# Two-layer language-model tower: when the latent loop sums and centres its query weights, and in which order MHA turns the halves of its probabilities

## The reference

```python
# MHA: 8 heads of width 128
q, k, v = x @ Wq + bq, x @ Wk + bk, x @ Wv + bv
attn = softmax(q @ k.T / sqrt(128));  out = concat(attn @ v) @ Wo
# latent: 8 groups x 16 heads, 100 latent positions in each
xn = l2norm(x) * gamma
q = xn @ Wq_w + Wq_b                       # 128 heads of width 128
qk = q @ kc.T / sqrt(128);  att = softmax(qk)   # over the 100 positions of kc
z = att @ vc;  zn = l2norm(z) * wz_g1
h1 = silu(zn @ wz_w1 + wz_b1);  out = silu(l2norm(h1) * wz_g2 @ wz_w2 + wz_b2)
```

## Time and profile before

| | us |
|---|---|
| median of 3 runs | 3082.61 (lowest 3079.25, highest 5605.95) |
| the profiled execution, its own time | 3107.84 |
| its span | 3106.0 |
| mean granted PE clock in it | 0.948 of full speed |
| MHA's steps in it | about 756 to 1290 us |
| the latent loop in it | about 1361 to 3106 us |

### The profile page before, as it was taken

The page is one execution under the profiler, slowest core; times in us unless marked ns, Lnnn a source line. Parts: engine busy times, 40 slices in busy tenths (PEclk is TensorE's granted clock), DMA queues, the critical chain, the costliest instruction groups (busy, mean ns, idle before and its releaser), DMA issues.

```text
span 3106.0 us, 44621 instructions
## 1 busy us (share of the span) xinstructions
PE 2780.7 (90%) x14652; PEld 2264.8 (73%) x14652; DVE 2293.7 (74%) x4039; ACT 1750.1 (56%) x3398; POOL 2094.3 (67%) x1520
## 2 busy tenths in 40 slices
PE   0569989696999999779999999999999999999996
PEld 0437666595888888568888888888777787788875
DVE  1459989535666666568888888888888888888875
ACT  0269978334656656435555655555555555555553
POOL 5369978103777777527777777777777776777763
PEclk7589999798999999879999999999999999999997
DMA  1011100000000000100111111011010100111100
GB/s 46 22 35 27 27 21 16 28 1 28 1 1 1 1 1 1 63 17 33 44 34 44 34 37 39 34 44 45 32 34 32 44 32 33 46 37 34 45 19 7
DMA packets 44693, 87.01 MB, mean 28 GB/s; under 512 B 10677, under 2 KB 24781, under 8 KB 43825
## 3 DMA queue, kind: packets, MB, share of 16 engines
q1 hardware_dynamic: 42928, 81.00, 8.0%
q0 software_dynamic: 1536, 3.15, 0.4%
HBM read 64.44 MB, written 1.05 MB: 21 GB/s over the span
## 4 chain that ended last, share of the span: by engine, by line
PE 39%; DVE 6%; POOL 6%; issue 4%; ACT 0%; POOLq 0%; ACTq 0%; DVEq 0%
PE lat_ps_h L2173 15%; PE lat_ps_z L2184 8%; PE lat_ps_s L2123 7%; PE lat_ps_t L2152 6%; POOL lat_zz L1800 3%; POOL lat_wq L1763 2%; PE lat_ps_s L2139 2%; PE lat_ps_s L2130 2%; DVE lat_wq_sum L1857 1%; DVE latm_sc L1837 1%; DVE latm_top L1832 1%; DVE latm_attT L1852 1%; DVE latm_tot L1844 1%; POOL latm_att L1787 0%; PE lat_ps_s L2206 0%
## 5 line engine op out<-in xcount | busy, mean ns | idle before, releaser
L1787 POOL TENSOR_TENSOR latm_att<-latm_sc,latm_tot 128x500 f32<-128x500 f32 (+1 forms) x416 | 421.4, 1013 | 460.6 <-DVE latm_tot L1846 450.1
L2173 PE MATMUL lat_ps_h<-latm_attT,lat_share 125*128 125x512 f32 (+1 forms) x2472 | 681.1, 407 | 34.8 <-DVE latm_attT L1852 31.7
L1800 POOL TENSOR_TENSOR lat_zz<-lat_zz,lat_zsq 128x512 f32<-128x512 f32 x508 | 655.3, 1290 | 20.0 <-ACT lat_zsq L2030 12.7
L2023 ACT CAST latm_attT<-lat_ps_t 125x512 fp32r<-125x512 f32 (+1 forms) x512 | 301.8, 589 | 620.8 <-PE lat_ps_t L2152 620.8
L2173 PEld LDWEIGHTS lat_ps_h<-latm_attT,lat_share 125*128 125x128 f32 (+1 forms) x2472 | 461.7, 189 | 160.5 <-DVE latm_attT L1852 54.8
L2184 PE MATMUL lat_ps_z<-latm_attT,lat_vc 100*128 100x512 f32 x1536 | 485.5, 424 | 0.2 <-ACT lat_zsq L2030 0.2
L995 POOL TENSOR_SCALAR mha_probs<-mha_probs,mha_inv 128x1024 f32<-128x1024 f32 x128 | 364.6, 2849 | 121.7 <-DVE mha_inv L1216 121.5
L1852 DVE TENSOR_TENSOR latm_attT<-lat_ps_t,latm_attT 125x512 fp32r<-125x512 f32 (+1 forms) x512 | 348.5, 681 | 107.3 <-ACT latm_attT L2023 107.0
L2123 PE MATMUL lat_ps_s<-lat_wk,lat_xr 128*128 128x500 f32 (+1 forms) x1248 | 353.0, 392 | 12.3 <-DVE latm_sc L1837 5.5
L457 POOL TENSOR_TENSOR ret_probs<-ret_probs,ret_shared 128x1024 f32<-128x1024 f32 x128 | 306.1, 2425 | 49.3 <-ACT ret_probs L590 49.3
L2152 PEld LDWEIGHTS lat_ps_t<-ident,latm_att 128*125 128x125 f32 (+1 forms) x2048 | 284.2, 175 | 63.7 <-POOL latm_att L1787 16.6
(11 more groups left out here) (366 smaller groups left out, 4812.3 us busy)
## 6 DMA issues: line engine op xcount, KB each, us to landing
lat_w_in<-in_w_fives SPq DMA_DIRECT2D x52, 640.0 KB, 4.2
lat_wq_in<-in_wq_fives SPq DMA_DIRECT2D x52, 320.0 KB, 2.9
lat_share<-lat_share SPq DMA_DIRECT2D x200, 50.0 KB
ret_qk_head<-ret_qk_parts SPq DMA_DIRECT2D x256, 32.0 KB, 2.0
moe_w<-in_W SPq DMA_DIRECT2D x2, 1024.0 KB, 4.8
ret_shared<-in_xpos_q SPq DMA_DIRECT2D x1, 1024.0 KB, 5.6
ret_shared<-in_xpos_k SPq DMA_DIRECT2D x1, 1024.0 KB, 4.8
latw_wkv<-in_Wkv SPq DMA_DIRECT2D x1, 1024.0 KB
```

What stands on the lines that cost most here:

```text
L1787: nc.gpsimd.tensor_tensor(att[:, k % SLOTS].rearrange("p (j l) -> p j l", j=QH)[:, 0:n, 0:L], sc[:, u, 0:n * L].rearrange("p (j l) -> p j ...
L1800: nc.gpsimd.tensor_tensor(dst, dst, zsq[:, n % 2], ALU.add).then_inc(s["zz_added"], 1)
L2173: mm = e.matmul(ps_h[:, f, c, :], share[0:w, q % 2, w_part, cols], attT[0:w, n % 2, a_part], start=(n % NS in (0, QH) and (a_part, w_part) ...
```

## The change

Nothing is added or left out of the computation; instructions and waits move. In MHA, `turn`, `high` and `low` go through the two halves in the order 1, 0 in every step that follows a piece of keys or values (all odd steps), and PE's wait for that piece stands ahead of half 0 alone. In the latent loop the sum is two steps after the scaling (step 5, where it was 4) and the centring three (step 6, where it was 5). For the last five the scaling is two steps earlier, so that its sum is one step earlier and its centring too.

```diff
--- before.py
+++ after.py
@@ -960,6 +960,7 @@
         chunk = lambda c: slice(c * BANK, (c + 1) * BANK)
         makes_keys = lambda step: (step // TB + 1, step % TB // 2 - 1) if step < K - TB and step % TB in (2, 4) else None
         makes_values = lambda step: ((step + 2) // TB, (step + 2) % TB // 2) if TB <= step + 2 < K and (step + 2) % TB in (0, 2) else None
+        halves_of = lambda k: (1, 0) if makes_keys(k + 1) or makes_values(k + 1) else (0, 1)
 
         def closes(step):
 
@@ -1051,8 +1052,14 @@
             def turn(k):
 
                 e.wait_ge(s["normed"], START + k + 1)
-                for half in range(2):
+                for half in halves_of(k):
                     e.wait_ge(s[f"low_ready{half}"], START + k)
+                    if half == 0 and makes_keys(k + 1):
+                        n, c = makes_keys(k + 1)
+                        e.wait_ge(s["keys_ready"], START + 2 * n + c + 1)
+                    if half == 0 and makes_values(k + 1):
+                        n, i = makes_values(k + 1)
+                        e.wait_ge(s["v_full_ready"], START + 2 * n + i + 1)
                     for j in range(4):
                         mm = e.transpose(psT[:, half, j * P:(j + 1) * P], probs[:, k % 4, (4 * half + j) * P:(4 * half + j + 1) * P], ident[:])
                     mm.then_inc(s["turned"], 1)
@@ -1100,12 +1107,6 @@
             for step in range(K + 14):
                 if LAG <= step < K + LAG:
                     gather(step)
-                if step >= 1 and makes_keys(step - 1):
-                    n, c = makes_keys(step - 1)
-                    e.wait_ge(s["keys_ready"], START + 2 * n + c + 1)
-                if step >= 1 and makes_values(step - 1):
-                    n, half = makes_values(step - 1)
-                    e.wait_ge(s["v_full_ready"], START + 2 * n + half + 1)
                 for b, c in adds_out(step - 1):
                     e.wait_ge(s["out_added"], START + 2 * b + c + 1)
                 if 2 <= step <= K + 1:
@@ -1145,8 +1146,8 @@
                 n, i = k // TB, k % TB
                 if i % 4 == 0 and n > 0:
                     e.wait_ge(s[f"spent{i // 4}"], START + n)
-                for half in range(2):
-                    e.wait_ge(s["turned"], START + 2 * k + half + 1)
+                for nth, half in enumerate(halves_of(k)):
+                    e.wait_ge(s["turned"], START + 2 * k + nth + 1)
                     e.copy(probsT[:, 0, 4 * half:4 * half + 4, i * P:(i + 1) * P], psT[:, half, :].rearrange("p (j s) -> p j s", j=4)
                            ).then_inc(s[f"high_ready{half}"], 1)
 
@@ -1659,7 +1660,7 @@
             for q in range(1, FIVES):
                 for i in range(len(pieces(q))):
                     share_at[begins[q - 1] + ((1, 3) if q == FIVES - 1 else (3, 4, 8) if full(q - 1) else (1, 2, 4))[i]] = (q, i)
-            wq_at = {(begins[q - 1] - 7 if q > 1 else 1 - LEAD): q for q in range(1, FIVES)}
+            wq_at = {(begins[q - 1] - (9 if q == FIVES - 1 else 7) if q > 1 else 1 - LEAD): q for q in range(1, FIVES)}
             vc_at = {begins[q - 1] + (1 if full(q - 1) and q < FIVES - 1 else -1): q for q in range(1, FIVES)}
             width = lambda n: ROWS if full(steps[n][0]) and steps[n][2] < QH - 1 else L
             pieces_before = lambda q: sum(len(pieces(i)) for i in range(q))
@@ -1815,8 +1816,8 @@
                         scale_vc(vc_at[n])
                     if n in wq_at:
                         scale_wq(wq_at[n])
-                    if n - 2 in wq_at:
-                        centre_wq(wq_at[n - 2])
+                    if n - 3 in wq_at:
+                        centre_wq(wq_at[n - 3])
                     for i, b, c in due(n, "spread"):
                         spread_norm(i, c)
 
@@ -1973,8 +1974,8 @@
                         total(k)
                     if 0 <= n + 1 < K:
                         low(n + 1)
-                    if n - 1 in wq_at:
-                        mean_wq(wq_at[n - 1])
+                    if n - 2 in wq_at:
+                        mean_wq(wq_at[n - 2])
                     if n == -LEAD:
                         e.tensor_tensor(w2[:], w2[:], g2[:].unsqueeze(2).to_broadcast([P, 2, D]), ALU.mult).then_inc(s["g2_scaled"], 1)
                     for i, b, half in due(n, "norm"):
```

## The result

The changed kernel takes **3051.85 us** (median of 4 runs, 3051.02 to 3054.51) where the kernel before took 3082.11: a ratio of 0.9908, 95% interval 0.9894 to 0.9922, so about 28 us less (24 to 33). Forecast were 42.5 us less. The direction holds, a third of the gain is missing. The profiled execution took 3051.48 us; its span is 3049.7.

A forecast was written before the change was run, and what follows sets the result against it. PE, busy for 90% of the span, was taken as the bound. Latent loop 23.0, clock 3.4, last five 6.4, first sum 2.1 and MHA 7.6 sum to 42.5 us off 3082.61: 3040 us, range 3022 to 3052.

The forecast's parts named there:

- the regular fives: Latent loop, 38 of 48 fives: step 6 loses its 0.76 us wait, step 7 loses 0.28, so 0.48 us saved each.
- The ten fives: Latent loop, fives with further DVE work in step 4: that work delays as before, so the same 0.48 us saved each.
- The clock: Latent loop: PE's clock no longer falls after the two waits of 1.82 us, saving 3.4 us.
- The last five: End of latent loop: PE's 4.5 us wait for query weights and 1.9 us of lower clock go, saving 6.4 us.
- The first sum: First sum of query weights: DVE's idle time ahead of it gets filled with 2.10 us of work, saving 2.1 us.
- MHA: Attention: transposes of half 1 go ahead of PE's wait for a piece, hiding 28 short waits and part of two: 7.6 us.
- Centring a step later: Latent loop, POOL: costs nothing, as centring ends before make_wk needs it, with 2.3 us left as cover.
- the wait moves whole: Rival, latent loop: step 6's wait moves whole to step 7, DVE being the bound; 3066 us, chance 0.10.
- L1859 isn't held up: Rival, latent loop: L1859 takes 0.17 us, not held by POOL; 15.8 us more saved, 3024 us, chance 0.13.
- the swap that gains nothing: Rival, MHA: swapping halves gains nothing because the score behind then waits for the exponential; 3048 us, chance 0.09.
- MHA's rival: Rival, MHA: the swapped halves gain nothing, the score behind waiting for the exponential; 3048 us, chance 0.09.

The follow-up runs named there:

- one_input: The changed kernel without the division by the width and the query bias in the sum, so that L1860 reads one input: 3033.62 us, ratio 0.9838.
- between: The changed kernel with DVE's sum of query weights moved, within step 5, from behind low(6) to between shift and total: 3043.39 us, ratio 0.9887.
- mha_only: The kernel before with only the change's MHA part, the swapped halves: 3072.12 us, ratio 0.9965.
- early_sum: The changed kernel with scaling, sum and centring of all but one five two steps earlier (steps 1, 3 and 4): 3029.58 us, ratio 0.9834.

## Why the prediction was wrong

**What bounds the kernel, and the regular fives: right.** The wait in step 6 went, the new loss is in step 7 (3.47 us for 3.49 forecast), and a five gained 0.51 us for 0.48. The 0.68 us of L1860 and its end with L1801 came as worked out, and `one_input` and `between` show by two ways what being held costs: without it a five lasts 31.50.

**The step that failed:** "That work, 0.6 to 1.3 us, delays step 5 as before, and step 7 then by as much, where before it delayed step 6. So the same difference of 0.48 us is left." The work's duration was taken over from a place where the sum stood ahead of it and POOL was through. Without the sum it starts about 1.8 us sooner (measured from `low(5)`), inside POOL's instructions, and is itself held: the root 15.9 us for 7.0, and in the four other fives L1932 1.65 us for 1.21, L1948 1.14 and 1.11 for 0.68, L1949 1.67 and 1.65 for 0.69. I had the measure of this in hand for L1859, and applied it to the one instruction that the diff moves, not to those that it exposes. L1883, L1884, L1932, L1948 and L1949 read two tensors in SBUF, as L1859 does, so the prediction's own reasoning on L1859 covered them. L1879 and L1880 read one. The Trainium skill, "SBUF — State Buffer", section "Who interferes with whom", lists `tensor_scalar` among the operations that can lock with GpSimd, which bears on L1879 and L1880, and says of `tensor_reduce` that on trn2 it never does. The traces agree with both (0.61 and 1.21 us ending with POOL's; 0.16 us in `one_input`).

The ten fives were to give 4.8 us and gave: six with root steps +5.8, the four others -1.5, so 4.3 us worse than before and 9.1 short. One more was overlooked: in five 26 the sum met an idle POOL before (the 0.17 us of the earlier trace rows), and now takes 1.05 us and ends with an L1801. It cost 1.0 us instead of gaining 0.48. The 38 "regular" ones were really 36, and with five 26 and 25 gave 17.5 us for 18.2.

**The clock: the level right, the gain not.** The windows at the places of the earlier trace rows that had 0.57 are at 1.00 now (2426 to 2440 and 2660 to 2680), for fives 34 and 41. Their gain with it was 0.63 and 0.72 us, though, and not 0.48 + 1.7: PE's one wait of 1.8 became two, of 1.48 and 0.97 us in five 34 and of 1.42 and 0.98 in 41, with DVE's longer work there. So of 23.0 + 3.4 us the loop gave 13.2 (17.9 less the last five's 4.7): 9.1 us are short in the ten fives, 3.4 in the clock's term, 0.7 in the others. MHA and the last five gave 1.6 and 1.8 us more than forecast, which leaves 42.5 - 32.7 = 9.8 us short in the traces. The waits of the ten were listed as one in the forecast (0.6 to 1.4 us in step 7, some 9 us in all); they are two in each, and 18.7 us in all.

**The last five: right**, 4.7 us there for the 4.5 of the wait, and 3.5 in the tail, for 1.9. The tail isn't to be trusted to the microsecond: in kernels without that wait it took 100.3 to 104.5 us, depending on where the clock falls at its later waits. **The first sum: right**, 2.07 us for 2.1. **MHA: right**, 9.2 us in the trace and 0.35% (0.22 to 0.47, so 7 to 15 us) by `mha_only`, for 7.6; the only waits for L1198 left are the two first. **Centring a step later cost nothing**: it began at 2292.74, 6.67 us after step 6, and the `make_wk` behind it ran without a wait at 2296.41.

Of the rivals, "the wait moves whole" is refuted by step 7's 3.47 us, "L1859 isn't held up" by its 0.68 us, and the swap that gains nothing by `mha_only`. None of them named what happened. That the time lies inside the range, 0.15 us from its far end of 3052, is luck: the range had been opened that far for MHA's rival, and another cause filled it.

## What to carry to other kernels

When an instruction is taken away from ahead of others, price these again at the moment at which they will now start: on DVE, against what POOL is running then. An instruction that may be held is best placed where the other engine must be idle, because it waits for this one's next result and has ended what it had before, or where its own engine has a pause to spare. Where all delays end in one step, PE's wait gets longer and may cost clock as well; here, spreading them over steps (`early_sum`, 0.9834) was worth more than making the sum alone short (`between`, 0.9887).
